# Sort passes written as engine loops, and GpSimd's waits in the SRC pass put on the group before

## The chip, the cores and the metric

One core of one Trainium2 chip. The metric is device time in microseconds (us) of one execution. The kernel is a hand-scheduled program: every engine (TensorE, VectorE, ScalarE, GpSimd, SyncE) runs its own list of instructions, and semaphores hold them together.

## What is computed

A graph network with 50,000 nodes of 256 features and 12,500 edges. Layer 0 gathers projected source rows, weighs them by a softmax over the edges of each destination, and sums them by destination; layer 1 takes for each `src` node the mean of the rows of its `dst` neighbours. After each layer comes a residual addition and a layer normalisation.

```python
h = x @ Wn.T + bn;  e = edge_attr @ We.T + be
a = leaky_relu(sum((h[src] + e) * attn, -1), 0.01)
a = exp(a - segment_max(a, dst)[dst]);  a = a / (segment_sum(a, dst)[dst] + 1e-16)
z = layernorm(x + relu(segment_sum(h[src] * a, dst)))
mean = segment_sum(z[dst], src) / max(count(src), 1)
out = layernorm(z + z @ W1.T + b1 + mean @ W2.T + b2)
```

## The kernel before

**Sizes.** Edges come in T = 100 tiles of P = 128, GT = 4 tiles make a group, Q = 25 groups. The dense stage has G = 98 groups of 512 nodes. DST = 0 and SRC = 1 name the two sort keys.

**Two sort passes.** Both the destinations and the sources must be put in order so that sums over equal keys become matrix products. A key is split into a low digit (256 values) and a high digit (HC = 196 values). First a histogram: VectorE (`onehots`, L816) and ScalarE (`high_onehots`) write one-hot rows of both digits for every tile, and TensorE (`sort`, L1281; the products are at L1264) counts them up in one bank. From its running sums (`starts`) comes the first slot of every key. Then the main loop: ScalarE copies the table of slots out of the bank (`table`, the COPY at L662; the names of the profile call it sel), TensorE adds the two tiles' counts to the bank (L1264, `count_tile`) and looks up the slots of each tile's keys in the copied table (L1319), with one-hot rows of the low digit that VectorE (`low_across`) and ScalarE (`upper_across`: Abs at L614, Relu at L619) made of a row that SyncE loads. VectorE picks the high digit's slot (`found_rank`), counts earlier equal keys within the tile, adds both (`ranks`, L857: rank_i) and GpSimd scatters the tile to its ranks (`scatter_order`, L484). FLIGHT = 6 of these scatters may be under way. In the second pass GpSimd does not scatter at once; it gathers the source rows of x for the first key's order (X, L475), of which the indices (idx_out, idx_src) come from work put between VectorE's groups ORDER_AT = 4 to 6. SyncE copies x to z_scratch in chunks beside all of it.

All of the sort's loops are Python loops, written out in full on each engine. Other stages use `steps` (L36): it writes the first `head` groups out, turns the middle into an engine loop with 4 groups in the body, and writes the rest out.

```python
def steps(eng, n, unroll, head, tail, body, apart=None):
    ...
        with eng.Fori(a, b) as m:
            for u in range(unroll):
                body(m * unroll + u, m, u)
```

**After the sorts.** The aggregation by destination (TensorE, VectorE and ScalarE with `by_dst` in `steps`, heads of 4, 4 and 8 groups) ends in GpSimd's scatters into z_scratch (L523). The dense stage takes 98 groups through layer 1's products. Near its end GpSimd starts the SRC pass: gathers of the z rows of a group of edges (xin, L475 under L543 to L548), and three groups later the scatter of the finished rows (yout, L478) to the output. In a step of this pass TensorE turns the gathered rows and sums the neighbours (L1478), multiplies with both weights (`products`, 32 matmuls at L1342), VectorE does statistics (L929) and carries the sums of a source over tile borders (`carry_sums`, L1068), and ScalarE normalises (yout, L577). TensorE's and GpSimd's lists are written out here; ScalarE and VectorE use `steps`.

The functions that the change touches, as they stand before:

Of the kernel before, what the change touches and what calls it, by code (L numbers as in the profile page):

```python
# [8 lines left out]
GT = 4  # L9
# [43 lines left out]
def build(nc, x, src, dst, edge_attr, Wn, bn, We, be, attn, W1, b1, W2, b2, out):  # L53
# [24 lines left out]
    with ExitStack() as ctx:  # L78
# [243 lines left out]

        def in_range(q, lo, hi):
            return not isinstance(q, int) or lo <= q < hi
# [110 lines left out]
        def _(pool):  # L435
# [125 lines left out]
        def _(act):  # L561
# [47 lines left out]
            gaps = [0]  # L609

            def gap(o, digits_in, scale, offset):

                gaps[0] += 1
                a.activation(o, digits_in, ACT.Abs, bias=offset, scale=scale).then_inc(s_gap, 1)  # L614
                return gaps[0]
# [5 lines left out]
            def high_onehots(k, q):  # L621
                n = k * Q + q
                wait(act, s_hotA, n - 1)
                at = [(GT * q + j, gap_hi[2 * (n % 2) + j // 2]) for j in (1, 3)]
                made = [gap(o, iota16[:, 0:HC], -1.0, dig_f[k][:, 1, t:t + 1]) for t, o in at]
                for (t, o), m in zip(at, made):
                    ins = is_zero(onehot_hi[:, t, :], o, m)
                ins.then_inc(s_hotA, 1)

            def upper_across(k, q):  # L630
                n = k * Q + q
                act.wait_ge(s_lb[n % 4], 16 * (n // 4 + 1))
                wait(act, s_look[k], GT * (q - 1))
                if k == SRC and q < 2:
                    act.wait_ge(s_look[DST], T)
                wait(act, s_lbA, n)
                made = gap(gap_low, lowB[n % 4], -1.0, slot_f[:, 1:2])
                is_zero(onehotT[n % 2][:, 1, :], gap_low, made).then_inc(s_lbA, 1)
# [9 lines left out]
            for k in (DST, SRC):  # L648
                if k == SRC:
                    act.wait_ge(s_add[DST], T)  # L650
                for q in range(Q):
                    high_onehots(k, q)
# [4 lines left out]
                upper_across(k, 0)  # L657
                act.wait_ge(s_seed, k + 1)
                for i in range(T // 2):
                    wait(act, s_add[k], 2 * i)  # L660
                    wait(act, s_look[k], 2 * (i - 1))
                    a.copy(table[i % 2].rearrange("p b c -> p (b c)"), bank[2][:, 0:2 * HC]).then_inc(s_tab, 1)  # L662
                    if i % 2 == 0 and i // 2 + 1 < Q:
                        upper_across(k, i // 2 + 1)
                    if k == SRC and i == 2 * ORDER_AT + 5:
                        store_sorted(DST)

# [83 lines left out]
        def _(dve):  # L751
# [64 lines left out]
            def onehots(k):  # L816
                if k == SRC:
                    dve.wait_ge(s_add[DST], T)
                for t in range(T):
                    ins = ts(onehot_lo[:, t, :], iota16[:], dig_f[k][:, 0, t:t + 1], None, ALU.is_equal)  # L820
                    if t % 2 == 0:
                        ts(onehot_hi[:, t, :], iota16[:, 0:HC], dig_f[k][:, 1, t:t + 1], None, ALU.is_equal)
                    if t % GT == GT - 1:
                        ins.then_inc(s_onehot, 1)
# [14 lines left out]
            def low_across(k, q):  # L839

                n = k * Q + q
                dve.wait_ge(s_lb[n % 4], 16 * (n // 4 + 1))
                wait(dve, s_look[k], GT * (q - 1))
                if k == SRC and q < 2:
                    dve.wait_ge(s_look[DST], T)
                ts(onehotT[n % 2][:, 0, :], lowB[n % 4], slot_f[:, 0:1], None, ALU.is_equal).then_inc(s_lbT, 1)

            def found_rank(k, t):
                dve.wait_ge(s_look[k], t + 1)
                o = bank[3 + t % 4][:, 0:HC]  # L850
                stt(o, iota_f[:, 0:HC], dig_f[k][:, 1, t:t + 1], o, ALU.is_equal, ALU.mult,
                    accum_out=found[:, t:t + 1]).then_inc(s_found[k], 1)

            def ranks(k, q):
                dve.wait_ge(s_found[k], GT * q + GT)
                s = slice(GT * q, GT * q + GT)
                v.tensor_tensor(rank_i[k][:, s], earlier[:, s], found[:, s], ALU.add).then_inc(s_rank, 1)  # L857

            def tiles(k, between):
                low_across(k, 0)  # L860
                for q in range(Q):
                    n = k * Q + q
# [3 lines left out]
                    keys = keyB[n % 4]  # L866
                    for j in range(GT):
                        t = q * GT + j
                        odd = j % 2
                        if 2 <= t < GT:  # L870
                            dve.wait_ge(s_lbT, n + 2)
                        else:
                            wait(dve, s_found[k], t - 3)
                        ins = stt(pair_junk[odd], keys[:, (j - odd) * P:(j + 1) * P], pay[:, t:t + 1, k],
                                  earlier_mask[:, 1 - odd:2, :].rearrange("p b c -> p (b c)"), ALU.is_equal, ALU.mult,
                                  accum_out=earlier[:, t:t + 1])
                        if j == GT - 1:
                            ins.then_inc(s_kbu, 1)
                        if t >= 2:
                            found_rank(k, t - 2)  # L880
                        if j == 1 and q + 1 < Q:
                            low_across(k, q + 1)
                    if q >= 1:
                        ranks(k, q - 1)
                found_rank(k, T - 2)
                found_rank(k, T - 1)
# [346 lines left out]
        def _(pe):  # L1233
# [28 lines left out]
            def count_tile(o, t):  # L1262
                for b in range(2):
                    ins = mm(o[:, b * HC:(b + 1) * HC], onehot_lo[:, t, b * P:(b + 1) * P], onehot_hi[:, t, :],  # L1264
# [16 lines left out]
            def sort(k, after):  # L1281
# [3 lines left out]
                for t in range(T):  # L1285
                    if t % GT == 0:
                        pe.wait_ge(s_onehot, k * Q + t // GT + 1)
# [230 lines left out]
```

## Time and profile before

| | |
|---|---|
| median of 3 runs | 1555.24 us (1553.36 to 1556.54) |
| profiled execution | 1551.7 us |
| its span, first to last instruction | 1548.2 us |
| mean granted TensorE clock | 0.904 |
| busy us in the span | PE 1198.5, PEld 1030.5, DVE 1067.6, ACT 767.5, POOL 746.3 |

PE is TensorE's products, PEld its weight loads, DVE VectorE, ACT ScalarE, POOL GpSimd, SP SyncE. A bracket at the end of a row of a timeline is the idle time of the engine before the row and what ended it; "issue" is time in which the engine waited for nothing that the profile shows.

### The profile page before, as it was taken

The page shows a single profiled execution, that of the slowest core. Times are in us where ns is not written, and L with a number is a line of the kernel's source. Part 1 is how long each engine was busy: PE and PEld are TensorE (multiplying, and loading weights), DVE is VectorE, ACT ScalarE, POOL GpSimd, SP SyncE. Part 2 cuts the span into 40 slices and gives each one's busy share as a digit, 9 for nine tenths or more (in the row PEclk, how much of TensorE's full clock was granted, in tenths as well). Part 3 has the DMA queues.
Part 4 walks back from the last instruction along what each step waited for, and adds up shares of the span by engine and source line. Part 5 has one row for each costly group of instructions (what it writes and reads, how often), then busy time and mean ns, then how long its engine had stood idle before and what let it go on. Part 6 is the DMA issues. An engine that isn't in the chain of part 4 may idle for free.

```text
span 1548.2 us, 24971 instructions
## 1 busy us (share of the span) xinstructions
PE 1198.5 (77%) x6537; PEld 1030.5 (67%) x6537; DVE 1067.6 (69%) x4021; ACT 767.5 (50%) x1718; POOL 746.3 (48%) x731
## 2 busy tenths in 40 slices
PE   4567667627602999994999999998996888888884
PEld 3456556626501888883888888787785777777773
DVE  8855567515568555553999999998898666666661
ACT  5543357314300444442777777676775344434442
POOL 1066660466660677775444410555533345655563
PEclk9898889969955999997999999999999888888897
DMA  7744348647599666665666676888884123223321
GB/s 218 215 103 108 97 98 253 191 131 234 169 279 328 112 91 98 97 78 120 218 233 240 235 247 237 271 295 287 294 288 159 59 86 98 80 88 94 88 81 46
DMA packets 118445, 261.09 MB, mean 169 GB/s; under 512 B 23531, under 2 KB 57148, under 8 KB 118360
## 3 DMA queue, kind: packets, MB, share of 16 engines
q1 hardware_dynamic: 76026, 194.08, 39.5%
q0 software_dynamic: 40128, 64.45, 18.8%
q10 hardware_dynamic: 2206, 1.57, 0.3%
q8 instruction: 35, 0.57, 0.2%
q14 instruction: 50, 0.41, 0.1%
HBM read 182.48 MB, written 130.49 MB: 202 GB/s over the span
## 4 chain that ended last, share of the span: by engine, by line
PE 41%; DVE 22%; issue 12%; another core or an unknown queue 7%; ACT 6%; POOL 6%; DMA 5%; ACTq 0%; DVEq 0%; POOLq 0%
PE bank L1342 19%; DVE stats L929 9%; PE bank L1319 8%; DVE xin L762 4%; PE bank L1331 4%; POOL out_rows L478 3%; DMA xin<-z_scratch,idx_src 3%; PE bank L1383 3%; PE bank L1387 3%; PE bank L1264 3%; POOL xin L475 2%; ACT aggn L614 2%; DVE xT L765 2%; DVE X L762 2%
## 5 line engine op out<-in xcount | busy, mean ns | idle before, releaser
L1342 PE MATMUL bank<-w1T,xT 128*128 128x256 f32 x1968 | 480.6, 389 | 16.7 <-ACT yout L577 14.7
L1342 PEld LDWEIGHTS bank<-w1T,xT 128*128 128x128 f32 x1968 | 372.6, 195 | 79.6 <-ACT yout L577 15.7
L484 POOL DMA_INDIRECT order_scratch<-pay,rank_i x200 | 195.0, 975 | 239.5 <-DVE rank_i L857 97.7
L577 ACT ACTIVATE yout<-bank,nmr,rstd 128x256 f32<-128x256 f32 x492 | 251.9, 577 | 1.3 <-DVE nmr L765 1.3
L568 ACT COPY xT<-bank 128x512 f32<-128x512 f32 x296 | 174.1, 589 | 145.9 <-PE bank L1331 87.4
L929 DVE BATCH_NORM_STATS2 stats<-xin 128x6 f32<-128x512 f32 x246 | 159.1, 690 | 84.9 <-DMA xin<-z_scratch,idx_src 63.2
L929 DVE BATCH_NORM_STATS2 stats<-bank 128x6 f32<-128x512 f32 x246 | 166.5, 686 | 65.1 <-PE bank L1342 47.7
L1264 PE MATMUL bank<-X 128*128 128x196 bf16 x800 | 102.0, 267 | 132.5 <-ACT sel L662 65.1
L523 POOL DMA_INDIRECT z_scratch<-xin,idx_out x100 | 156.6, 1566 | 99.6 <-ACT xin L688 76.5
L765 DVE SCALAR_TENSOR_TENSOR bank<-iota_f,dig_f,bank 128x196 f32<-128x196 f32 x200 | 85.2, 426 | 152.3 <-PE bank L1319 77.7
L1264 PEld LDWEIGHTS bank<-X 128*128 128x128 bf16 x800 | 70.4, 105 | 166.8 <-ACT sel L662 77.0
L572 ACT ACTIVATE std<-stats,eps_c 128x4 f32<-128x4 f32 x271 | 82.9, 307 | 197.0 <-DVE stats L929 168.1
L1319 PE MATMUL bank<-sel,agg 128*128 128x196 f32 x800 | 172.2, 364 | 0.1
L478 POOL DMA_INDIRECT out_rows<-yout,idx_out x100 | 99.8, 998 | 147.8 <-issue 59.8
L475 POOL DMA_INDIRECT X<-z_scratch,idx_dst x100 | 95.0, 950 | 142.6 <-DVE xin L762 111.4
L1331 PE MATMUL bank<-ident,xin 128*128 128x128 f32 x984 | 138.4, 281 | 20.4 <-DVE xin L762 19.6
L1319 PEld LDWEIGHTS bank<-sel,agg 128*128 128x128 f32 x800 | 148.1, 213 | 0.7 <-DVE bank L765 0.3
L475 POOL DMA_INDIRECT X<-in_x,idx_src x100 | 96.9, 969 | 99.6 <-DVE idx_out L916 52.1
L1331 PEld LDWEIGHTS bank<-ident,xin 128*128 128x128 f32 x984 | 120.9, 147 | 31.2 <-issue 21.4
L762 DVE TENSOR_SCALAR xin<-xin,nmr,rstd 128x256 f32<-128x256 f32 x392 | 136.3, 412 | 0.1
L1342 PE MATMUL bank<-w2T,agg 128*128 128x256 f32 x400 | 121.4, 433 | 0.0
L475 POOL DMA_INDIRECT xin<-z_scratch,idx_src x100 | 96.2, 962 | 50.9 <-issue 30.8
(230 smaller groups left out, 1744.8 us busy)
## 6 DMA issues: line engine op xcount, KB each, us to landing
z_scratch<-in_x SPq DMA_DIRECT2D x125, 400.0 KB
xin<-z_scratch SPq DMA_DIRECT2D x97, 512.0 KB
out_rows<-yout SPq DMA_DIRECT2D x97, 512.0 KB
yout<-keys_scratch SPq DMA_DIRECT2D x50, 256.0 KB
kB<-sorted_scratch SPq DMA_DIRECT2D x50, 256.0 KB
yout<-low_digits_scratch SPq DMA_DIRECT2D x50, 128.0 KB
xin<-in_edge_attr SPq DMA_DIRECT2D x12, 512.0 KB, 5.4
order_scratch<-pay,rank_i POOLq DMA_INDIRECT x200
```

The costliest lines, as they stand in the source:

```text
L475: g.indirect_dma_start(out=dst_ap, out_offset=None, in_=table, in_offset=where).then_inc(s, 16)
L478: g.indirect_dma_start(out=table, out_offset=where, in_=src_ap, in_offset=None, bounds_check=N - 1, oob_is_err=False).then_inc(s, 16)
L484: g.indirect_dma_start(out=order_dram[k], out_offset=bass.IndirectOffsetOnAxis(ap=rank_i[k][:, t:t + 1], axis=0), in_=pay[:, t, :], in_off ...
L523: g.indirect_dma_start(out=z_dram, out_offset=column(idx_out[DST], GT * q + j), in_=xin[q % 4][:, j, :], in_offset=None, compute_op=ALU.ad ...
L568: a.copy(xT[dst_i][:].rearrange("p a b c -> p (a b c)"), src_bank[:, :]).then_inc(copied, 1)
L577: a.activation(yout[hu][0:rows, j, :], bank_of(j // 2)[0:rows, (j % 2) * D:(j % 2 + 1) * D], ACT.Identity, bias=nmr[0:rows, slot, j:j + 1] ...
L762: return v.tensor_scalar(o, i, s1, s2, o0, o1) if o1 is not None else v.tensor_scalar(o, i, s1, s2, o0)
L929: return v.bn_stats(stats[0:rows, slot, 2 * p:2 * p + 2, :].rearrange("p j s -> p (j s)"), pair.rearrange("p j c -> p c j"))
L1264: ins = mm(o[:, b * HC:(b + 1) * HC], onehot_lo[:, t, b * P:(b + 1) * P], onehot_hi[:, t, :], start=False, stop=False, skip_group_check=True)
L1319: ins = mm(bank[3 + t % 4][:, 0:HC], onehotT[n % 2][:, b, j * P:(j + 1) * P], table[i % 2][:, b, :], start=b == 0, stop=b == 1)
L1331: ins = tr(o[:, at:at + n], buf[0:n, 2 * p + jj, c * P:(c + 1) * P], ident[0:n, 0:n])
L1342: ins = mm(to, buf[:, jj, c, 0:n], w[:, c, :], start=not bias and i == 0 and c == 0, stop=i == len(terms) - 1 and c == 1)
```

## The change

Two things are done together. The sort's Python loops on TensorE, VectorE and ScalarE become `steps` loops, with a head of 4 groups (8 in the second pass's main loop) and a tail of 1: five, or four, rounds of a body with 4 groups. Numbers that were known when the program was written (semaphore values, tile addresses) become values in registers in the looped groups. The instructions, their tiles and their order are the same. In GpSimd's SRC pass the wait for the gathers of the same group ahead of the scatters is taken out; a wait for the gathers of the group before stands ahead of each group of gathers, and a wait for the scatters of the group before ahead of each group of scatters.

```diff
+        def ring_at(k, m, u):
+            return (k * Q + u) % 4, m + (k * Q + u) // 4
+        def row_of(buf, t):
+            return buf[:, bass.ds(t, 1), :].rearrange("p a c -> p (a c)")
...
             for q in range(Q + 3):
                 if q < Q:
+                    if q >= 1:
+                        pool.wait_ge(s_xs[(q - 1) % 4], 16 * GT * ((q - 1) // 4 + 1))
...
                     pool.wait_ge(s_ey, GT * h + GT)
-                    if q < Q:
-                        pool.wait_ge(s_xs[q % 4], 16 * GT * (q // 4 + 1))
+                    if h >= 1:
+                        pool.wait_ge(s_ysc[(h - 1) % 4], 16 * GT * ((h - 1) // 4 + 1))
...
-                for q in range(Q):
-                    high_onehots(k, q)
+                steps(act, Q, 4, 4, 1, lambda q, m, u: high_onehots(k, q, u))
...
-                for i in range(T // 2):
-                    wait(act, s_add[k], 2 * i)
-                    wait(act, s_look[k], 2 * (i - 1))
-                    a.copy(table[i % 2].rearrange("p b c -> p (b c)"), bank[2][:, 0:2 * HC]).then_inc(s_tab, 1)
-                    if i % 2 == 0 and i // 2 + 1 < Q:
-                        upper_across(k, i // 2 + 1)
+                def tables(q, m, u):
+                    for half in range(2):
+                        wait(act, s_add[k], 4 * q + 2 * half)
+                        wait(act, s_look[k], 4 * q + 2 * half - 2)
+                        a.copy(table[half].rearrange("p b c -> p (b c)"), bank[2][:, 0:2 * HC]).then_inc(s_tab, 1)
+                        if half == 0 and in_range(q, 0, Q - 1):
+                            upper_across(k, q + 1, m, u + 1)
...
+                steps(act, Q, 4, 4 + 4 * k, 1, tables)
...
+                def group(q, m, u):
+                    for j in range(GT):
+                        t = q * GT + j
+                        ins = ts(row_of(onehot_lo, t), iota16[:], dig_f[k][:, 0, bass.ds(t, 1)], None, ALU.is_equal)
...
+                steps(dve, Q, 4, 4, 1, group)
...
-                for q in range(Q):
-                    n = k * Q + q
-                    for f in between.get(q, ()):
+                def group(q, m, u):
+                    known = isinstance(q, int)
+                    for f in between.get(q, ()) if known else ():
                         f()
-                    dve.wait_ge(s_kb[n % 4], 16 * (n // 4 + 1))
+                    b, turn_no = ring_at(k, m, u)
+                    dve.wait_ge(s_kb[b], 16 * turn_no + 16)
...
+                steps(dve, Q, 4, 8 if between else 4, 1, group)
...
+                def count_group(q, m, u):
+                    pe.wait_ge(s_onehot, k * Q + q + 1)
+                    pe.wait_ge(s_hotA, k * Q + q + 1)
+                    for j in range(GT):
+                        count_tile(hist, q * GT + j)
+                steps(pe, Q, 4, 4, 1, count_group)
...
+                def look_up(q, m, u):
+                    for half in range(2):
+                        pe.wait_ge(s_tab, k * T // 2 + 2 * q + half + 1)
+                        for j in (2 * half, 2 * half + 1):
+                            count_tile(tab, q * GT + j).then_inc(s_add[k], 1)
...
+                steps(pe, Q, 4, 4 + 4 * k, 1, look_up)
```

## Rows read from the trace of the kernel before

**Rows 1.** The page's chain that ended last, shares by engine.

```profile
PE 41%; DVE 22%; issue 12%; another core or an unknown queue 7%; ACT 6%; POOL 6%; DMA 5%; ACTq 0%; DVEq 0%; POOLq 0%
```

**Rows 2.** Windows: us, then busy (x) of PE, PEld, DVE, ACT, POOL, clock, DMA.

```profile
218.20:254.50 36.30, 23.63 (x202) 18.99 (x202) 30.22 (x155) 36.23 (x102) 8.52 (x9) 0.86 0.79 244
...
341.00:430.00 89.00, 61.73 (x361) 54.21 (x361) 51.34 (x274) 32.80 (x58) 58.74 (x61) 0.90 0.65 189
76.00:222.00 146.00, 96.66 (x569) 85.14 (x568) 80.15 (x433) 56.53 (x103) 92.89 (x95) 0.90 0.39 96
```

**Rows 3.** Timeline, second sort pass, GpSimd idle: start, us, engine, line.

```profile
271.16 0.16 DVE L857 TENSOR_TENSOR rank_i<-earlier,found 128x4 int32<-128x4 f32 x1
...
275.02 0.17 DVE L857 TENSOR_TENSOR rank_i<-earlier,found 128x4 int32<-128x4 f32 x1
...
272.89 0.72 ACT L614 ACTIVATE aggn<-yout,slot_f 128x512 bf16<-128x512 bf16 x1 [0.92 <-PE bank L1319]
```

**Rows 4.** Timeline, first sort pass, a pair of groups: VectorE, GpSimd, ScalarE.

```profile
102.27 0.16 DVE L857 TENSOR_TENSOR rank_i<-earlier,found 128x4 int32<-128x4 f32 x1
...
114.47 0.16 DVE L857 TENSOR_TENSOR rank_i<-earlier,found 128x4 int32<-128x4 f32 x1
...
111.69 0.96 POOL L484 DMA_INDIRECT order_scratch<-pay,rank_i  x1 [0.30 <-issue]
114.91 0.96 POOL L484 DMA_INDIRECT order_scratch<-pay,rank_i  x1 [2.26 <-DVE rank_i L857]
...
114.21 0.49 ACT L662 COPY sel<-bank 128x392 f32<-128x392 f32 x1 [4.49 <-remote]
```

**Rows 5.** Timeline, second sort pass: GpSimd's first and last of 39 gathers; VectorE.

```profile
286.66 1.02 POOL L475 DMA_INDIRECT X<-in_x,idx_src  x1 [52.09 <-DVE idx_out L916]
...
335.31 0.94 POOL L475 DMA_INDIRECT X<-in_x,idx_src  x1 [0.30 <-issue]
...
335.10 0.43 DVE L765 SCALAR_TENSOR_TENSOR bank<-iota_f,dig_f,bank 128x196 f32<-128x196 f32 x1 [9.68 <-remote]
```

**Rows 6.** Timeline of GpSimd, aggregation by destination: first scatters of groups.

```profile
520.21 1.56 POOL L523 DMA_INDIRECT z_scratch<-xin,idx_out  x1 [1.42 <-ACT xin L688]
...
544.94 1.61 POOL L523 DMA_INDIRECT z_scratch<-xin,idx_out  x1 [1.08 <-ACT xin L688]
...
553.19 1.56 POOL L523 DMA_INDIRECT z_scratch<-xin,idx_out  x1 [1.03 <-ACT xin L688]
...
577.92 1.56 POOL L523 DMA_INDIRECT z_scratch<-xin,idx_out  x1 [1.08 <-ACT xin L688]
```

**Rows 7.** Chain of the whole span: its piece in the first histogram.

```profile
11.76 28.47 DVE X L762 x150
```

**Rows 8.** Timeline of GpSimd, a step of the SRC pass.

```profile
1303.78 1.01 POOL L478 DMA_INDIRECT out_rows<-yout,idx_out  x1 [3.89 <-DMA xin<-z_scratch,idx_src]
...
1309.00 0.99 POOL L475 DMA_INDIRECT xin<-z_scratch,idx_src  x1 [0.30 <-issue]
...
1317.23 1.01 POOL L478 DMA_INDIRECT out_rows<-yout,idx_out  x1 [3.46 <-DMA xin<-z_scratch,idx_src]
```

**Rows 9.** Chain in three stretches of the SRC pass: start, us, what.

```profile
1226.43 8.60 PE bank L1342 x32
...
1240.24 5.92 PE bank L1342 x20
...
1420.71 8.60 PE bank L1342 x32
...
1434.38 8.60 PE bank L1342 x32
...
1251.32 5.54 another core or an unknown queue
```

**Rows 10.** Timeline of GpSimd: first and last of 16 gathers at the dense end.

```profile
1160.27 0.95 POOL L475 DMA_INDIRECT xin<-z_scratch,idx_src  x1 [17.84 <-PE bank L1331]
...
1181.92 0.95 POOL L475 DMA_INDIRECT xin<-z_scratch,idx_src  x1 [0.30 <-issue]
```

More of the change, by code:

```diff
@@ L619, in is_zero, with high_onehots, upper_across @@
                 return a.activation(o, gap_in, ACT.Relu, bias=ones[:, 0:1], scale=-1.0)
-            def high_onehots(k, q):
-                n = k * Q + q
[L623 to L627, printed above, removed]
+            def high_onehots(k, q, u):
+                wait(act, s_hotA, k * Q + q - 1)
+                at = [(GT * q + j, gap_hi[2 * ((k * Q + u) % 2) + j // 2]) for j in (1, 3)]
+                for t, o in at:
+                    gap(o, iota16[:, 0:HC], -1.0, dig_f[k][:, 1, bass.ds(t, 1)])
+                for i, (t, o) in enumerate(at):
+                    ins = is_zero(row_of(onehot_hi, t), o, 3 * Q * k + 2 * q + 1 + i)
                 ins.then_inc(s_hotA, 1)
-            def upper_across(k, q):
-                n = k * Q + q
-                act.wait_ge(s_lb[n % 4], 16 * (n // 4 + 1))
+            def upper_across(k, q, m, u):
+                b, turn_no = ring_at(k, m, u)
+                act.wait_ge(s_lb[b], 16 * turn_no + 16)
                 wait(act, s_look[k], GT * (q - 1))
-                if k == SRC and q < 2:
+                if k == SRC and isinstance(q, int) and q < 2:
                     act.wait_ge(s_look[DST], T)
-                wait(act, s_lbA, n)
-                made = gap(gap_low, lowB[n % 4], -1.0, slot_f[:, 1:2])
-                is_zero(onehotT[n % 2][:, 1, :], gap_low, made).then_inc(s_lbA, 1)
+                wait(act, s_lbA, k * Q + q)
+                gap(gap_low, lowB[b], -1.0, slot_f[:, 1:2])
+                is_zero(onehotT[b % 2][:, 1, :], gap_low, 3 * Q * k + 2 * Q + q + 1).then_inc(s_lbA, 1)
             def dense_copy(h, h_par, p):
@@ L1304, in sort @@
                    skip_group_check=True).then_inc(s_seed, 1)
-                for q in range(Q):
-                    n = k * Q + q
-                    for i in range(GT * q // 2, GT * q // 2 + GT // 2):
-                        pe.wait_ge(s_tab, k * T // 2 + i + 1)
-                        for t in (2 * i, 2 * i + 1):
-                            count_tile(tab, t).then_inc(s_add[k], 1)
-                        if 2 * i == GT * q:
-                            pe.wait_ge(s_lbT, n + 1)
-                            pe.wait_ge(s_lbA, n + 1)
-                        for t in (2 * i, 2 * i + 1):
-                            wait(pe, s_found[k], t - 3)
-                            j = t % GT
+                def look_up(q, m, u):
[3 more added lines that the diff above has]
+                            count_tile(tab, q * GT + j).then_inc(s_add[k], 1)
+                        if half == 0:
+                            pe.wait_ge(s_lbT, k * Q + q + 1)
+                            pe.wait_ge(s_lbA, k * Q + q + 1)
+                        for j in (2 * half, 2 * half + 1):
+                            wait(pe, s_found[k], q * GT + j - 3)
                             for b in range(2):
-                                ins = mm(bank[3 + t % 4][:, 0:HC], onehotT[n % 2][:, b, j * P:(j + 1) * P], table[i % 2][:, b, :],
-                                         start=b == 0, stop=b == 1)
+                                ins = mm(bank[3 + j][:, 0:HC], onehotT[(k * Q + u) % 2][:, b, j * P:(j + 1) * P],
+                                         table[half][:, b, :], start=b == 0, stop=b == 1)
                             ins.then_inc(s_look[k], 1)
-                    if q in after:
+                    if isinstance(q, int) and q in after:
                         after[q]()
+                steps(pe, Q, 4, 4 + 4 * k, 1, look_up)
                 nothing(tab, start=False, stop=True)
```

71 lines of the change are left out of this document (30 added, 41 removed).

## The prediction

> **What bounds the kernel now.** I read the page's chain first. TensorE holds 41% of it, VectorE 22%, but 7% is "another core or an unknown queue", on a single core [rows 1]. So I cut the span into stages [rows 2] and read in each the chain and the engines' timelines, to see which wait ends last. The change touches the two sort passes (76 to 222 and 257 to 430 us), the histogram before the second (218 to 254.5), the SRC pass (1202 to 1507) and, through GpSimd's first four groups of gathers, the end of the dense stage.
>
> The second sort pass shows its unhindered pace while GpSimd is idle: rank additions at 271.16 and 275.02, 3.86 us for a group of four tiles [rows 3]. No engine is full there. It is a ring: ScalarE's Abs at 272.89 has waited 0.92 us for TensorE's look-ups [rows 3]; behind it come its Relu and its copy of the table, then TensorE's counts, the look-ups, VectorE's pick of the slot, and ScalarE again.
>
> Elsewhere the sort is much slower. The first pass takes 146 us for 25 groups, 5.84 each, with GpSimd busy 92.89 [rows 2]. One pair of groups shows why [rows 4]: ranks at 102.27 and 114.47, 12.20 us for two groups. GpSimd scatters 8 tiles back to back, the last at 111.69, and is then idle 2.26 us for a rank at 114.91. Meanwhile ScalarE's copy at 114.21 has waited 4.49 us for something that the profile cannot name. What waits for TensorE gets its signal late while GpSimd issues indirect transfers without a pause, and soon after the run ends. In the second pass the same is larger: GpSimd gathers from 286.66 to 335.31 with hardly a pause, and VectorE sits idle 9.68 us until 335.10 [rows 5]. After that 89 us go by for the 15 or 16 groups that are left, 5.6 to 5.9 each [rows 2].
>
> **The change, part by part.** Profiled time 1551.7 us, span 1548.2, so 3.5 around it; the median of three runs is 1555.24, 3.5 above the profiled one. I add to 1551.7 and carry the sum to the median.
>
> Part one turns the sort's groups into engine loops: the same instructions, tiles and increments, but semaphore values and tile addresses come from registers. Four groups stay in front (eight in the second pass's main loop) and one behind, so each engine takes 4+4+4+3 = 15 branches back. No row of the sort shows such a loop. The nearest is the aggregation by destination, where TensorE and VectorE run groups 0 to 3 written out and loop from group 4. GpSimd's scatters there start at 520.21 and 544.94 written out, and 553.19 and 577.92 looped: 24.73 us for three groups both times [rows 6]. So a loop costs nothing where its engine's queue is ahead of its work; lower bound nothing. But there TensorE is the full engine. In the sort every engine waits for another once or more per ring, and register arithmetic that was hidden ahead of a wait now may lie behind it. Four look-up tiles and four counts, each with a computed address, and three register waits on ScalarE stand in the ring. The only row-borne price of an instruction step is the 0.30 us that the timelines put between two of GpSimd's issues [rows 4]; one or two such steps in a ring of 3.86 give 0.3 to 0.6. I estimate 0.5, an unhindered group of 4.4 us (range 3.9 to 5.0).
>
> **Histogram, second pass.** ScalarE runs without a gap, 36.23 busy of 36.30 us [rows 2], so each of 25 groups costs 1.45 us. Here no wait sits in front, so only decode counts: +0 to +0.2 us for each of 20 looped groups, +0 to +4; I take +2. The first histogram is bound by VectorE's 150 one-hots, 28.47 us of the chain at 0.19 each [rows 7], also a stream with no wait in front: 0 to +2, in the range; I take 0.
>
> **First pass, main loop.** A pair of groups costs 12.2 us: GpSimd's run of 8 plus a part in which the ring must turn to give it new ranks. Only the turning part, about two groups, is longer: 2 x 0.5 = +1 us for each of the 10 looped pairs, **+10**. The bound below: eight scatters at 1.26 take 10.1, so if slower ranks broke the run up and signals came in time, a pair could fall from 12.2 to 10.1: 10 x 2.1 = -21. The bound above: 1.1 us a group, +22.
>
> **Second pass.** GpSimd's backlog run is the same transfers, so its 49 us stay. Before it four to six groups are written out. Of the 16 looped ones some 13 lie after 341 us, where GpSimd already sets part of the pace (58.74 of 89 us busy [rows 2]); I take 0.3 each, **+4** (-7 to +14).
>
> What stands after the sorts hides nothing: the copy of z fills the DMA engines once the last group is done, so those 16 us go on to the end one for one.
>
> Part two is on GpSimd in the SRC pass. In a step it scatters four tiles (1303.78 on), gathers four (from 1309.00), waits 3.46 us for their landing and scatters again at 1317.23: 13.45 us with no other idle time [rows 8]. The wait that is removed is this 3.5 to 3.9. The new waits (gathers of the group before, scatters of the group before) come after at least 5 us of other issue and have landed, since a landing takes 3.5 to 3.9. So GpSimd's own ring falls to some 4 x 1.3 + 4 x 1.27 + the release of yout, about 12.3 at most. But another ring of the same length stands beside it [rows 9]: TensorE's 32 products 8.60 us at 1226.43, VectorE's statistics, the carry of the sums, TensorE's turn, and the next products at 1240.24: 13.81. Later 1434.38 starts the next products after 13.67. GpSimd is no part of it. Hence a step stays at 13.4 to 13.8 and the gain is some 0.2 in about 10 steps, -2. Against it stands one doubt: where GpSimd now issues eight in a row more often, the late signals of [rows 4] can come back: the chain holds 5.54 us of "an unknown queue" at 1251.32, in this pass too [rows 9]. I take **-1** (-15 to +15).
>
> The same wait splits the first 16 gathers, now from 1160.27 to 1181.92 nearly without a pause [rows 10], into fours with a landing of 3 to 4 us between. A run of 8 cost a waiting engine 4.49 us in [rows 4]; here one of 16 lies over the last dense groups, and the pauses should end what it costs: 0 to -5, I take **-3**. The last of these gathers starts later by 3 x 3.5 = 10 us, near 1192; the SRC pass reads the first group only from 1202, so this stays covered; without the cover it would cost these 10 us once.
>
> Sum: +2 +10 +4 -1 -3 = +12: 1563.7 by the profiled execution, 1567 by the median; 1566 to keep a little of the room below.
>
> **A rule against the loops.** The by-destination loop of [rows 6] shows no branch cost at all. The Trainium skill (page "Runtime: NRT & Kernel Launch", section "Instruction fetch mechanics") says that a taken branch to a target outside the two pages held must fetch before going on, and that this is why kernels prefer full unrolling. By that rule the 15 branches of an engine could each cost one fetch from memory; this case's rows have no such fetch, the nearest being the landing of a gather, 3.9 us [rows 8]: 15 x 3.9 = 58 us, or about 1613. The rows of the loop that exists speak for 0, so I give it 3 in 100, inside case B below.
>
> **The rivals.**
> A, the forecast: the ring gets slower by its address arithmetic, the SRC pass hardly moves. 1558 to 1580, centre 1566.
> B, more than that: the arithmetic costs over 1 us a group (20 x 1.1 in the first pass, 13 x 1.1 in the second, +4: +40), or a loop refetches, or the late signals spread in the SRC pass. For it: the ring crosses engines five times. Against: [rows 6]. 1580 to 1615.
> C, faster: ranks that come slower and evenly break GpSimd's runs of eight, so its late-signal stall (2.26 us a pair of idle GpSimd, 4.49 of idle ScalarE) vanishes. The place is the pair in [rows 4]; it decides from the point where the ring plus the stall is shorter than the run of 10.1 us. 10 pairs x 2.1 = -21 and -7 in the second pass, with -3 to -4 from the dense end: 1525 to 1548. Or GpSimd's wait was what held all steps of the SRC pass: 13.5 to 12.9 for 22 steps is -13, 1542. For it: before the run of gathers the ring reached 3.86, so the engines can. Against: TensorE's and VectorE's own 13.7.
> D, no change to be measured: the registers are computed ahead of the waits as in [rows 6], or small costs cancel. 1552 to 1558.
>
> **How the numbers follow.** A 0.44, B 0.16, C 0.27, D 0.13. A measurement of this kernel tells 0.2%, 3.1 us, from no change. Likeliest: A, 1566. Range: C's far half (below 1538) and B's far part (above 1591) are left out, about 2 in 10: 1538 to 1591; A's own range is 1558 to 1580. Faster is C with a little of D's edge, 0.28; same 0.13; slower A and B, 0.59.
>
> **What would show it.** In the changed profile: rank additions in the second pass 3.86 apart in the written-out groups and 4.2 to 5 in looped ones while GpSimd is idle; pairs in the first pass 13.2 instead of 12.2; the second histogram's 25 groups still in 36 to 40 us; in the SRC pass scatters released by ScalarE's yout instead of by the gathers' landing, with products 13.5 to 13.8 apart; the gathers from 1160 on in fours. Wrong would make it: pairs below 12 us (C), branches with idle stretches of over 1 us at every fourth group (B), or steps of the SRC pass below 13 us, which would mean that the ring of [rows 9] was itself held by GpSimd.

## The result and the profile after

Five executions of the changed kernel took 1590.18 us in the median (1569.58 to 1591.13), five of the kernel before 1553.36 (1545.68 to 1556.54): a ratio of 1.0203, 95% interval 1.0166 to 1.0241. It is slower, as forecast, but by 37 us and not by 11: the time lies in case B, just inside the range. Ratios here and below leave out executions more than 1.5% above the fastest of their kernel, so where single executions spread that far a ratio lies below the quotient of the medians. The profiled execution is the fastest of the five, 1569.58 us, so its trace holds only half of the loss.

The windows of the changed kernel, with columns as in [rows 2]: TensorE's second histogram from its start to its end (227.7 to 279.7), the first pass, and the second pass under and after GpSimd's long run.

```profile
227.70:279.70 52.00, 38.45 (x204) 20.48 (x202) 30.61 (x156) 36.57 (x101) 9.37 (x10) 0.68 0.63 197
76.80:229.00 152.20, 106.65 (x565) 87.79 (x562) 78.94 (x421) 53.62 (x96) 91.10 (x92) 0.89 0.36 91
311.40:364.00 52.60, 16.52 (x73) 13.38 (x72) 12.68 (x69) 6.92 (x12) 35.53 (x38) 0.63 0.50 148
364.00:457.40 93.40, 70.19 (x374) 55.98 (x372) 52.87 (x280) 32.98 (x58) 59.52 (x62) 0.93 0.65 190
```

The ranks (VectorE, L866 now) in the timeline: last of the first pass, first two of the second, last of the second.

```profile
229.00 0.16 DVE L866 TENSOR_TENSOR rank_i<-earlier,found 128x4 int32<-128x4 f32 x1
...
292.11 0.15 DVE L866 TENSOR_TENSOR rank_i<-earlier,found 128x4 int32<-128x4 f32 x1
295.97 0.16 DVE L866 TENSOR_TENSOR rank_i<-earlier,found 128x4 int32<-128x4 f32 x1
...
457.26 0.16 DVE L866 TENSOR_TENSOR rank_i<-earlier,found 128x4 int32<-128x4 f32 x1
```

Before, ranks at the same four places stood at 220.90, 267.31, 271.16 and 429.14. So the first pass ends 8.1 us later, the stretch between the passes takes 63.1 instead of 46.4 (+16.7), and the second pass 165.15 instead of 161.83 (+3.3). In its written-out groups the ring still turns in 3.86, against [rows 3]. In the first pass the groups from the ninth to the twenty-second rank went from 6.13 us each (126.62 to 206.33) to 6.71 (129.90 to 217.15), 1.2 for two groups where I had put 1. All of the surprise of the sort is in the middle, where I had put +2. The timeline of TensorE in the second histogram shows it:

```profile
231.60 0.85 PE L1276 MATMUL bank<-X 128*128 128x196 bf16 x8 [0.22 <-issue]
...
239.17 1.49 PE L1276 MATMUL bank<-X 128*128 128x196 bf16 x8 [5.58 <-DVE X L768]
...
249.03 6.93 PE L1276 MATMUL bank<-X 128*128 x32 [0.59 <-ACT X L623]
256.47 6.82 PE L1276 MATMUL bank<-X 128*128 x32 [0.50 <-ACT X L623]
...
268.93 1.51 PE L1276 MATMUL bank<-X 128*128 x8 [0.20 <-issue]
...
272.75 6.55 PE L1276 MATMUL bank<-X 128*128 x32 [0.21 <-issue]
```

Written out, eight counting products take 0.85 us. In the loop 32 take 6.8, 0.21 each, and a round of four groups 7.44 (249.03 to 256.47), 1.86 a group, where ScalarE needs 1.40 to 1.45. TensorE, which had room, is now the slowest of the three: its last product ends at 279.3, ScalarE's last one-hot at 267.6. The granted clock is lower here as well, but it is not what sets this pace. Eight looped products take 1.51 us at a granted clock of 1.00 (at 268.93). At 0.50, four times eight take 6.82 (at 256.47), which is 1.7 each with the 0.2 between them. Eight written out take 0.85 at 1.00 and 1.49 at 0.50 (at 231.60 and 239.17). One more thing stretches the stage. VectorE's one-hots, 0.19 apart otherwise, come up to 1.4 apart under GpSimd's last scatters, and TensorE waits 5.58 us for them (at 239.17):

```profile
235.63 0.31 DVE L768 TENSOR_SCALAR X<-iota,dig_f 128x256 bf16 x1 [1.11 <-issue]
237.02 0.27 DVE L768 TENSOR_SCALAR X<-iota,dig_f 128x196 bf16 x1 [1.08 <-issue]
...
239.12 0.29 DVE L768 TENSOR_SCALAR X<-iota,dig_f 128x256 bf16 x1 [1.10 <-issue]
240.53 0.27 DVE L768 TENSOR_SCALAR X<-iota,dig_f 128x196 bf16 x1 [1.12 <-issue]
```

GpSimd's run of 12 transfers without a break ended at 239.2; the next one-hots from 241.25 on come at their old pace. Under the run of the kernel before, the gaps were 0.43 at most. But it is not the loop that makes them: in the kernel whose second histogram is written out on all three engines (below) VectorE has them too, and TensorE stands idle there for 3.57 us.

```profile
240.84 0.47 DVE L773 TENSOR_SCALAR X<-iota,dig_f 128x256 bf16<-128x256 bf16 x2 [1.11 <-issue]
...
245.10 1.05 DVE L773 TENSOR_SCALAR X<-iota,dig_f 128x256 bf16<-128x256 bf16 x5 [1.12 <-issue]
```

Written out, TensorE makes such a delay good (64 products in 8.52 us from 245.21); looped, it cannot.

From the sort's end on the profiled execution wins back 8.5 us of its 28. GpSimd's gathers at the dense end begin at 1186.03, 25.8 us after [rows 10]; the last instruction is 19.6 later than before, so some 6 us come after that point. From the first of these gathers to the first scatter of the SRC pass it takes 54.55 us instead of 58.11 (-3.6, where I had put -3), and from there to the first of the last four scatters 311.3 instead of 313.9 (-2.6, where I had put -1). The 16 gathers now come in fours, 1186.03, 1192.93, 1200.90 and 1208.25, and the SRC pass repeats every 13.6 us, as in [rows 9]: the chain has its 32 products there.

```profile
1317.18 7.65 PE bank L1355 x32
1330.82 7.65 PE bank L1355 x32
1344.46 7.68 PE bank L1355 x32
```

### The profile page after: what moved, and what is told of

Read it like the earlier page. It is cut to its first block, busy times and chain, and to the rows that moved or that the text cites. A ratio compares the mean times of both kernels' runs of the same rounds, so it can differ in the third digit from the quotient of the medians.

```text
span 1567.8 us, 27460 instructions
## 1 busy us (share of the span) xinstructions
PE 1244.1 (79%) x6537; PEld 1041.7 (66%) x6537; DVE 1068.1 (68%) x4021; ACT 765.1 (49%) x1718; POOL 747.0 (48%) x731
## 4 chain that ended last, share of the span: by engine, by line
PE 56%; issue 12%; DVE 11%; ACT 8%; another core or an unknown queue 6%; DMA 4%; POOL 2%; ACTq 1%; SPq 0%; DVEq 0%; POOLq 0%
PE bank L1355 29%; PE bank L1331 7%; PE bank L1344 7%; PE bank L1276 5%; DVE stats L941 5%; PE bank L1396 3%; PE bank L1400 3%; ACT aggn L619 2%; DVE xT L771 2%; PE bank L1491 2%; ACT yout L586 2%; DVE xin L768 1%; ACT X L623 1%; DMA xin<-z_scratch,idx_src 1%
## 5 line engine op out<-in xcount | busy, mean ns | idle before, releaser
L1355 PE MATMUL bank<-w1T,xT 128*128 128x256 f32 x1968 | 468.4, 383 | 12.9 <-ACT yout L586 11.1
L1355 PEld LDWEIGHTS bank<-w1T,xT 128*128 128x128 f32 x1968 | 366.4, 192 | 72.1 <-ACT yout L586 13.9
L1276 PE MATMUL bank<-X 128*128 (+1 forms) x800 | 141.8, 286 | 122.8 <-ACT sel L667 63.6
L1276 PEld LDWEIGHTS bank<-X 128*128 (+1 forms) x800 | 79.1, 103 | 191.0 <-issue 141.4
L1331 PE MATMUL bank<-sel,agg 128*128 128x196 f32 x800 | 176.2, 369 | 1.4
L1344 PE MATMUL bank<-ident,xin 128*128 128x128 f32 x984 | 143.1, 287 | 20.8 <-DVE xin L768 19.6
L1344 PEld LDWEIGHTS bank<-ident,xin 128*128 128x128 f32 x984 | 125.1, 150 | 32.1 <-issue 21.4
```

The lines of the kernel that those rows point to most:

```text
L1276: ins = mm(o[:, b * HC:(b + 1) * HC], row_of(onehot_lo[:, :, b * P:(b + 1) * P], t), row_of(onehot_hi, t), start=False, stop=False, skip_g ...
L1331: ins = mm(bank[3 + j][:, 0:HC], onehotT[(k * Q + u) % 2][:, b, j * P:(j + 1) * P], table[half][:, b, :], start=b == 0, stop=b == 1)
L1344: ins = tr(o[:, at:at + n], buf[0:n, 2 * p + jj, c * P:(c + 1) * P], ident[0:n, 0:n])
L1355: ins = mm(to, buf[:, jj, c, 0:n], w[:, c, :], start=not bias and i == 0 and c == 0, stop=i == len(terms) - 1 and c == 1)
```

## The experiments

Eighteen runs, each beside fresh executions of the kernel before on the same chip. Two kinds of chip were met, which the table keeps apart by the time of the kernel before: 1562 to 1567 us, near the 1553 of the comparison above (chips 2 and 10), and 1423.5 us (chips 15 and 4). "Not met" means that the kernel was not run on that kind.

| kernel | before 1562 to 1567: ratio (interval) | before 1423.5: ratio (interval) |
|---|---|---|
| the change | 1.0384 (1.0306 to 1.0463), 1.0344 (1.0274 to 1.0413), 1.0256 (1.0173 to 1.0339) | not met |
| loops alone | 1.0189 (1.0132 to 1.0247) | not met |
| new waits alone | none given; 1568 to 1621 and 1561 to 1632 us | not met |
| landing wait at every second group | 1.0289 (1.0215 to 1.0362) | 1.0004 (0.9993 to 1.0014) |
| change, second histogram written out | 1.0399 (1.0338 to 1.0461) | not met |
| loops, TensorE's counting written out | 1.0104 (1.0045 to 1.0163) | not met |
| loops on TensorE alone | not met | 1.0126 (1.0100 to 1.0151), 1.0136 (1.0110 to 1.0162) |
| loops on ScalarE and VectorE alone | not met | 1.0010 (0.9997 to 1.0024), 1.0012 (0.9999 to 1.0026) |
| pauses at the dense end alone | not met | 0.9999 (0.9988 to 1.0009), 1.0005 (0.9993 to 1.0018) |
| pauses in GpSimd's x gathers | 1.0110 (1.0054 to 1.0167) | 1.0372 (1.0351 to 1.0393) |

The new waits alone have no ratio, because their single executions lie 53 to 70 us apart.

**The change again, and its halves.** The loops alone keep GpSimd's part of the kernel before; the waits alone are GpSimd's two edits in the kernel before.

> The changed kernel once more, since its five times lie at 1569.6 and at 1587 to 1591. Theory 1 (the sort pays for register arithmetic and for what GpSimd's transfers do to it, and how GpSimd's long runs fall against the groups differs between executions): 1570 to 1591, and a slower profile shows its extra time between 77 and 460 us. Theory 2 (the extra time of the slower executions is in the dense stage or the SRC pass, at a lower granted clock): the sorts end at 457 us as in the profile shown, and the rest is longer.

> The sort as loops alone, GpSimd's waits in the SRC pass as before the change. Theory 1 (the loops cost all, 17 us in the second histogram, 8.5 and 3.5 in the two main loops, and GpSimd's waits give back about 8): 1578 to 1598, 1.5 to 3% above the kernel before. Theory 2 (GpSimd's waits cost time in the usual execution): 1568 to 1578, faster than the change as a whole.

> GpSimd's new waits alone, the sort written out. Theory 1: the profile of the change is 8 us shorter from the dense stage's end on than the kernel before, so 1543 to 1550, ratio 0.994 to 0.998. Theory 2 (the waits do nothing by themselves): 0.998 to 1.002. Steps of the SRC pass stay near 13.6 us in both.

Measured, in the median: 1633.98, 1592.18 and 1607.93 us beside 1562.1. The loops cost 30 us, as expected and evenly from one execution to the next (1584 to 1596). My theory 1 of the waits, a gain, fell: they cost between 6 and 59 us. The change came out above the 1570 to 1591 of theory 1, and theory 2 had the place right: of the 80 us that its profiled execution (1649.35) lies above the first one, 57.5 are in the SRC pass (368.8 us from the first scatter to the first of the last four, against 311.3), and the sort ends 10 us later. The chain of the waits-alone kernel in the SRC pass shows a step's worth:

```profile
1352.67 2.52 DMA xin<-z_scratch,idx_src
...
1356.28 0.68 DVE stats L931
1356.96 9.53 another core or an unknown queue
...
1372.46 2.56 PE bank L1344 x6
```

and GpSimd's timeline around it:

```profile
1343.62 1.02 POOL L478 DMA_INDIRECT out_rows<-yout,idx_out  x1 [6.68 <-ACT yout L579]
...
1352.67 0.94 POOL L475 DMA_INDIRECT xin<-z_scratch,idx_src  x1 [0.30 <-issue]
1354.23 1.02 POOL L478 DMA_INDIRECT out_rows<-yout,idx_out  x1 [0.61 <-issue]
...
1363.26 0.94 POOL L475 DMA_INDIRECT xin<-z_scratch,idx_src  x1 [0.30 <-issue]
```

The next yout is already there when four gathers end, and since nothing makes GpSimd wait for their landing it issues 16 transfers in one run, 1343.62 to 1364.2. Under it VectorE waits 9.53 us for a signal. The profile does not name its sender; by the program it is TensorE, whose last product for it had ended at 1357.1. All of the pass stalls, and behind the stall the same comes again: steps of 15 to 19 us. In the profile of the change above the runs were 8 long and the steps 13.6. Both patterns are in one binary, and which one an execution falls into differs.

**Is it the removed wait or the added ones?**

```diff
-                    if q < Q:
+                    if q < Q and q % 2 == 0:
                         pool.wait_ge(s_xs[q % 4], 16 * GT * (q // 4 + 1))
```

> The kernel before, with the wait for the landing ahead of the scatters kept in every second group only, no new waits. GpSimd can then issue 16 transfers in a row instead of 8. Theory 1 (the landing wait is what keeps GpSimd's runs short, and a run of 16 delays the signals of TensorE that VectorE and ScalarE wait for): slower in some or all executions, 1.005 to 1.03, with steps of 15 to 19 us where the runs are 12 or longer. Theory 2 (the loss comes from the two new waits): within 0.3% of the kernel before.

> The kernel before with the landing wait at every second group of the SRC pass only; once within 0.1% on the chip where nothing is late. Theory 1 (run length of GpSimd): between no wait removed and all removed, 1.005 to 1.03, where signals are late; 0.999 to 1.001 where not. Theory 2 (the loss is in the new waits themselves): within 0.3% on either.

> GpSimd's new waits alone. Theory 1: within 0.3% of the kernel before on a chip where nothing is late (steps stay 13.6 us, TensorE's and VectorE's ring), 1.01 to 1.04 with steps of 15 to 19 us where signals are late. Theory 2 (GpSimd's landing wait did hold the steps): 0.985 to 0.995 where nothing is late.

The first met a chip where the kernel before takes 1423 us: 1.0004, no loss, so its expectation was missed. The second met one with 1567 us: 1.0289, with nothing added. The missing landing wait is enough. Its trace has the same pattern: 16 transfers in one run from 1312.72 to 1333.8, and in the chain a piece of 9.21 us without a name at 1326.60. The waits alone repeated their spread, on the same kind of chip as before.

**What the second kind of chip is.** The same kernel before is 130 to 143 us faster there. Four fifths of that lie ahead of the adds into z, which start at 404.97 instead of 511.49. Windows of the kernel with pauses at the dense end, whose sort is that of before; the first and second pass:

```profile
77.40:167.80 90.40, 83.38 (x565) 74.78 (x562) 76.06 (x421) 53.52 (x96) 67.61 (x70) 1.00 0.69 153
214.50:305.40 90.90, 84.39 (x572) 75.70 (x570) 77.87 (x433) 51.65 (x90) 52.25 (x54) 1.00 0.85 259
```

90.4 us for the first pass instead of 143.7: its ranks are 3.86 apart, through runs of dozens of GpSimd's transfers, at TensorE's full granted clock (1.00, against 0.90 in [rows 2] and 0.63 under the long run above). The chains of all eight traces taken there hold no piece of "an unknown queue"; in the twelve others, those of the comparison included, it has 3 to 11%. So the late signals of [rows 4] do not follow from the program alone; they belong to a kind of chip, as far as four chips tell, none of which was met in both ways. The comparison that I forecast was made on that kind.

**The loops, engine by engine.**

```diff
-                steps(pe, Q, 4, 4, 1, count_group)
+                written_out(pe, Q, 4, 4, 1, count_group)
...
-                steps(pe, Q, 4, 4 + 4 * k, 1, look_up)
+                written_out(pe, Q, 4, 4 + 4 * k, 1, look_up)
```

`written_out` runs the same body in a Python loop. The other kernel has it at the four loops of ScalarE and VectorE.

> The sort as loops on ScalarE and VectorE, TensorE's part written out, GpSimd's waits as before. Theory 1 (most of the loss of the loops, 30 us when they are all there, is TensorE's issue: 0.21 us for each looped product of the histogram, its address arithmetic between the wait and the look-ups in the main loops): 1.003 to 1.008. Theory 2 (the loss is in the waits of ScalarE and VectorE): 1.012 to 1.02.

> The sort as loops on TensorE alone, GpSimd's waits as before. Theory 1: 1.010 to 1.018, the second histogram 12 us longer than 34, ranks in the main loops about as with all loops. Theory 2: under 1.006.

> Loops on ScalarE and VectorE alone, GpSimd's waits as before; 1.0010 where nothing is late. Theory 1 (register arithmetic of these engines is cheap except where GpSimd's run delays it): 1.002 to 1.008 where signals are late. Theory 2 (they carry half of the loss there): 1.010 or more.

> Loops on TensorE alone, GpSimd's waits as before; 1.0126 where nothing is late, with ranks 4.42 us apart instead of 3.86. Theory 1: 1.010 to 1.018 where signals are late too, of which about 10 us are the second histogram. Theory 2 (late signals hide what the loop costs in the main loops): 1.005 to 1.008.

All four met chips where nothing is late, which gives the clean price. The first one without TensorE's loops came out at 1.0010, below the 1.003 that I expected at least. Ranks of the loops on TensorE alone, in the timeline of the first pass:

```profile
101.67 0.15 DVE L869 TENSOR_TENSOR rank_i<-earlier,found 128x4 int32<-128x4 f32 x1
106.06 0.15 DVE L869 TENSOR_TENSOR rank_i<-earlier,found 128x4 int32<-128x4 f32 x1
110.46 0.16 DVE L869 TENSOR_TENSOR rank_i<-earlier,found 128x4 int32<-128x4 f32 x1
114.88 0.15 DVE L869 TENSOR_TENSOR rank_i<-earlier,found 128x4 int32<-128x4 f32 x1
119.29 0.16 DVE L869 TENSOR_TENSOR rank_i<-earlier,found 128x4 int32<-128x4 f32 x1
```

4.39 to 4.42 us a group, my estimate of 4.4, at a granted clock of 1.00. With TensorE written out and the other two looped it is 3.93 (100.78, 104.71, 108.66): if the two prices add, seven eighths is TensorE's. The timeline of the looped kernel also says where: after ScalarE's copy TensorE idles 0.49 us before its four counts and takes 0.75 for them, against 0.30 and 0.51 in the sort written out.

```profile
101.64 0.75 PE L1279 MATMUL bank<-X 128*128 x4 [0.49 <-ACT sel L670]
```

The end of the second pass is 27.9 us later than in the kernel with TensorE's part as it was (333.35 against 305.42): +11.3 in the first pass, +8.3 between the passes, +9.0 in the second, less 0.6 at the start. But the kernel loses only 19: there GpSimd's gathers, not the sort, set when the adds into z start (420.29 against 404.97).

**The counting by itself.** The first line of the diff above alone; and, in the full change, all three engines' loops of the second histogram.

> The change, but with the second histogram written out on the three engines. Theory 1 (each of TensorE's 160 looped counting products there costs 0.21 us instead of 0.10, so the counting ends 12 us behind ScalarE, and GpSimd's scatters hold the register arithmetic of ScalarE and VectorE for 5 us): the histogram takes 34 us instead of 50, and the kernel is 14 to 18 us faster than the change. Theory 2 (the counting falls behind because of the transfers beside it, not because of the loop): the histogram still takes 45 us or more, gain under 5.

> All loops of the sort, but with TensorE's counting in both histograms written out; GpSimd's waits as before. Theory 1 (TensorE's looped counting at 0.21 us a product is 8 to 12 us of the loops' loss): 8 to 12 us faster than all loops, so 1.010 to 1.014 where signals are late (all loops 1.019) and about 1.006 to 1.009 where not. Theory 2 (counting in the loop is hidden under ScalarE's one-hots): as all loops.

With TensorE's counting alone written out the loops cost 1.0104 on one chip, instead of 1.0189 on another: some 13 us less, as expected, though the intervals touch. The stretch itself is the better measure. From the last rank of the first pass to the first of the second it takes 49.3 us against 60.8 with all loops:

```profile
240.00:289.30 49.30, 33.17 (x247) 26.34 (x248) 37.52 (x188) 38.94 (x103) 6.29 (x7) 0.86 0.70 223
```

```profile
234.00:294.80 60.80, 46.73 (x247) 29.27 (x248) 37.54 (x186) 38.45 (x101) 7.46 (x8) 0.72 0.55 178
```

TensorE is 46.73 us busy there for the same 247 products that take 33.17. The whole histogram written out in the full change gave 47.8 us for that stretch; its total, 1619.94, is 14 below the change on the same chip, though the SRC pass swings by as much.

**Run length in the sort.** GpSimd's x gathers and the dense end with pauses:

```diff
+                if t % GT == 0 and 0 < t <= 44:
+                    pool.wait_ge(s_xg[(t - 1) % FLIGHT], 16 * ((t - 1) // FLIGHT + 1))
                 wait(pool, s_xg[t % FLIGHT], 16 * (t // FLIGHT))
```

> The kernel before, with GpSimd pausing for the landing of each four of its first 44 gathers of x rows under the second sort pass, and of each four at the dense end. Theory 1 (a run of more than about five transfers makes TensorE's signals late, runs of four do not): where signals are late the sort's ranks come 3.9 to 4.5 us apart under the gathers instead of standing still for 29 to 43 us, the sort ends 40 to 60 us sooner, the adds into z start 25 to 40 us sooner, ratio 0.975 to 0.985. Theory 2 (late signals depend on the transfers' number or on the copies of x beside them, not on the runs): the sort stands still as before, and GpSimd ends later, ratio 1.00 to 1.02. Where no signal is late: GpSimd's gathers end about 25 us later and the ratio is 1.00 to 1.02.

> GpSimd pauses for the landing of each four of its first 44 gathers of x rows, and at the dense end; 1.037 where no signal is late, since there GpSimd's gathers simply end later. Where signals are late, theory 1 (runs of more than about five transfers are the cause): ranks 3.9 to 4.5 us apart under the gathers instead of a standstill of 29 to 43 us, the sort ends 40 to 60 us sooner, ratio 0.975 to 0.99. Theory 2 (the number of transfers, or the copies beside them): the standstill remains and the ratio is 1.01 to 1.04.

Where signals are late (before 1562.08) the timeline of VectorE under the paused gathers has

```profile
308.35 0.15 DVE L861 TENSOR_TENSOR rank_i<-earlier,found 128x4 int32<-128x4 f32 x1
312.29 0.16 DVE L861 TENSOR_TENSOR rank_i<-earlier,found 128x4 int32<-128x4 f32 x1
317.78 0.16 DVE L861 TENSOR_TENSOR rank_i<-earlier,found 128x4 int32<-128x4 f32 x1
320.97 0.16 DVE L861 TENSOR_TENSOR rank_i<-earlier,found 128x4 int32<-128x4 f32 x1
```

and the window from 292 to 345 is full, where [rows 5] had a standstill:

```profile
292.00:345.00 53.00, 45.51 (x307) 40.42 (x307) 43.05 (x237) 29.47 (x51) 21.68 (x23) 1.00 0.85 245
```

The second pass took 97.5 us instead of 165 (271.40 to 368.89), near the 90.9 of the other kind of chip. In the window ScalarE waits 2.8 us in all for something without a name. So runs of four hardly delay signals and long ones do: theory 1 of the mechanism holds. That it is the length of a run, and not the slower rate of transfers that the pauses also bring, is not separated by this run. The forecast of the time fell all the same, 1.011 and not 0.98. A pause lasts 3.3 to 6.9 us, GpSimd's gathers end at 477, and in the three kernels with the written-out sort and no pauses at 436 to 440; the adds into z start at 543.33 instead of 519.8 to 523.0. The wait moved from the sort to GpSimd. On the other kind of chip there is nothing to win and the same pauses cost 3.7%.

**The dense end, and the change once more.**

```diff
                 if q < Q:
+                    if 1 <= q < 4:
+                        pool.wait_ge(s_xs[q - 1], 16 * GT)
```

> The kernel before, with one thing of the change: GpSimd waits for the landing of each of the first three groups of gathers at the end of the dense stage before it starts the next. The wait for the landing inside the SRC pass stays. Theory 1 (the new order of waits loses in the SRC pass and gains only at the dense end): 2 to 6 us faster, ratio 0.996 to 0.999, and no step of the SRC pass of 16 us or more beyond the one or two of before. Theory 2 (the pauses at the dense end start what goes wrong later): slower, steps of 15 to 19 us.

> The kernel before with the pauses at the dense end only; on a chip where nothing is late 0.9999. Theory 1: where signals are late 3 to 6 us faster, 0.996 to 0.998, steps of the SRC pass 13.6 us but for one or two. Theory 2 (a shifted start of the SRC pass starts the long steps): 1.01 or more.

> The changed kernel. Two kinds of chip have been met: on one the kernel before takes 1555 to 1562 us and signals of TensorE come late under GpSimd's runs; on the other it takes 1423 and none are late. Theory 1 (loops cost issue time on both kinds; GpSimd's new waits cost only where signals are late): 1.015 to 1.03 on a chip of the second kind, 1.02 to 1.05 on one of the first. Theory 2 (the change loses only by late signals): within 0.5% on a chip of the second kind.

> The changed kernel. Theory 1 (loops cost issue time on both kinds of chip, GpSimd's new waits only where signals are late): 1.012 to 1.020 where nothing is late, ranks 4.4 us apart in the looped groups, steps of the SRC pass 13.6 us; 1.02 to 1.05 where signals are late. Theory 2 (the change loses only by late signals): within 0.5% where nothing is late.

The pauses at the dense end change nothing where nothing is late, so the 0.996 to 0.999 of the first expectation was missed. They met no chip of the other kind alone, but the traces there bear out my -3 in place: from the first of the 16 gathers to the first scatter of the SRC pass it takes 53.8 to 56.5 us in the eight traces with pauses, and 58.1 to 61.5 in the four without. The change stayed 2.6 to 3.8% slower where signals are late; what it costs on the other kind of chip was not met. No version that was run beats the kernel before.

## Why the prediction was off

The sum had five terms.

The main loops were right. I gave the ring +0.5 us a group and measured +0.55 with TensorE looped, on a chip without late signals (4.41 against 3.86). I gave the first pass +10 and the second +4. The profiled execution has +8.5 and +3.3; over the later traces on chips with late signals the first pass takes 157 to 164 us looped and 147.5 to 150 written out, the second 166 to 168 and 165 to 166. In the second pass GpSimd's run covers most of the price, as I argued: +9.0 where nothing is late, against +3.3 here.

The histogram's +2 is the step that failed: 16.7 in the profile, and 13 in the later traces (58.2 to 60.9 us from pass to pass against 44.2 to 49.4). I bounded it by ScalarE, "here no wait sits in front, so only decode counts: +0 to +0.2 us for each of 20 looped groups", and asked for the engine that was full. TensorE has eight products a group there, each with addresses of both operands from registers; at some 0.10 us more for each that is 0.8 a group, which takes it past ScalarE's 1.45. I priced an instruction step at 0.30 us for the ring and then did not multiply it by the number of instructions in a stream. The loop that I took for comparison, [rows 6], could not show this: its products take 0.22 us each (four in 0.87 from 522.72), so a pace of 0.19 to 0.21 hides behind them. The rest of the term is the hold-up of VectorE under GpSimd's run, 1.4 us between two one-hots instead of 0.19, which a written-out TensorE makes good. That the 0.10 is the arithmetic of the addresses, and not the loop as such, is argued: no run loops the counting with fixed addresses.

The SRC pass, -1, failed in some executions and not in others. "A step stays at 13.4 to 13.8" is what the profiled execution did. But "where GpSimd now issues eight in a row more often" named the danger and sized it too small: the removed wait was what ended GpSimd's runs, without it they reach 16. From its first scatter to the first of its last four the pass took 313.9 us before and 312.6 and 313.1 with the loops and the old waits; with the new waits it took 321 to 381 in six later traces, and 346 where only every second landing wait was removed. With the loops' 28 to 30 us it accounts for the spread of the change between 1570 and 1649. That the four unprofiled executions of the comparison, 1587 to 1591, got their extra 17 to 22 us in that pass is argued from this, not shown.

The dense end's -3 was right where it was placed: -3.6 in the profile.

Of rival C's mechanism the first half came true: slower ranks did break GpSimd's runs, from eights one after another to 4, 4, 8, 4, 4, 8 (from 103.54 on). The second half did not: after an eight GpSimd was now idle up to 4.3 us (before 130.33, for instance) instead of 2.2, and the pass grew. Case B was right in the outcome and in one of its three causes, the late signals. Its 15 refetches did not come: on the chip without late signals the ranks go through every round of TensorE's loop 4.39 to 4.47 us apart (4.28 to 4.61 in the second such run), with no step at each fourth group (the five shown above cover a whole round). The Trainium skill (page "Runtime: NRT & Kernel Launch", section "Instruction fetch mechanics") gives a fetch after a taken branch whose target is outside the two pages held as a reason to write loops out. By these rows the branches cost nothing that can be seen, so its condition may not have been met; no run shows where the targets lie.

## What to carry to other kernels

Before a written-out stream becomes an engine loop, count the instructions in it that take an address from a register, and add the price to each engine of the stage and not only to the one that is full: some 0.10 us for each of TensorE's short products turned an engine that was idle for a third of the stage into the slowest. Before a wait is moved on GpSimd, ask what its runs of indirect transfers look like without it; a wait that looks like waste may be the pause that others need. And a pause put in elsewhere has to be paid by an engine that has the time.

## What the runs showed of the hardware

The same program takes 1423.5 us on some chips and 1553 to 1567 on others. Four fifths of the difference lie ahead of the adds into z, and one thing is seen on the slower kind only. While GpSimd issues indirect transfers every 1.25 to 1.3 us, signals that by the program are TensorE's reach VectorE and ScalarE late: by 4.49 us under a run of 8 and 9.53 under one of 16. The longest piece without a name in the chain of the changed kernel has 23.16 us (at 336.53, under the second pass's gathers).

Under such runs other engines also issue more slowly what waits for nothing: 1.1 us pass between two one-hots of VectorE, looped or written out, and TensorE's written-out transposes in the SRC pass come 1.41 apart (1359.38 and 1360.79 in the waits-alone kernel).

Runs of four with a landing between them do little harm. A looped product of TensorE with both addresses from registers takes 0.19 us at a granted clock of 1.00, one written out 0.11. What makes a chip one kind or the other is not known from these runs.
